# An expert stage whose residual, scaling and final sum move to other engines

## The reference, cut to what matters

```python
x = _layernorm(x + sa, g1, beta1)
t = x.reshape(-1, D)                                  # 1250 x 512
idx = jnp.argmax(t @ Wg + bg, axis=-1)                # one of 8 experts per token
h = jax.nn.gelu(jnp.einsum('td,edh->teh', t, W1) + b1, approximate=False)   # 512 -> 256
y = jnp.einsum('teh,ehd->ted', h, W2) + b2                                  # 256 -> 512
moe = jnp.einsum('ted,te->td', y, one_hot(idx, E))
return _layernorm(x + moe, g2, beta2)                 # and the caller adds x of the stage before
```

## Time and profile before

| | |
|---|---|
| median of 3 runs | 1898.34 us (1892.71 to 1900.72) |
| the profiled execution's own time | 1899.85 us |
| its span | 1898.2 us |
| PE busy | 1765.4 us (93% of the span) |
| PEld busy | 1537.4 us (81%) |
| DVE busy | 1307.2 us (69%) |
| ACT busy | 913.3 us (48%) |
| POOL busy | 591.2 us (31%) |
| the expert stage, from its first load to the end | about 1785.9 to 1898.2 us |

### The profile page before, as it was taken

The page is one execution under the profiler, slowest core; times in us unless marked ns, Lnnn a source line. Parts: engine busy times, 40 slices in busy tenths (PEclk is TensorE's granted clock), DMA queues, the critical chain, the costliest instruction groups (busy, mean ns, idle before and its releaser), DMA issues. The chain is left out here.

```text
span 1898.2 us, 31991 instructions
## 1 busy us (share of the span) xinstructions
PE 1765.4 (93%) x10970; PEld 1537.4 (81%) x10970; DVE 1307.2 (69%) x2964; ACT 913.3 (48%) x1660; POOL 591.2 (31%) x532
## 2 busy tenths in 40 slices
PE   7998999799999999999689999999899999999596
PEld 5776899688888888788578998988688888888585
DVE  6444466688888888377665565545588787887776
ACT  4332266577777776222331243324465555555421
POOL 0000102555556552011101212222254545444344
PEclk9999999899999999999899999999899999999798
DMA  7652677877777775667222049875020202112632
GB/s 246 213 196 77 203 240 250 221 200 204 201 204 198 203 204 142 156 169 186 86 78 73 1 131 162 203 207 182 11 44 1 66 7 58 32 32 71 217 123 89
DMA packets 183532, 265.14 MB, mean 140 GB/s; under 512 B 55852, under 2 KB 102443, under 8 KB 181109
## 3 DMA queue, kind: packets, MB, share of 16 engines
q1 hardware_dynamic: 117839, 169.58, 30.9%
q0 software_dynamic: 49920, 62.94, 12.4%
q10 hardware_dynamic: 15640, 30.90, 6.6%
HBM read 198.55 MB, written 85.86 MB: 150 GB/s over the span
## 5 line engine op out<-in xcount | busy, mean ns | idle before, releaser
L1103 POOL DMA_INDIRECT edge_rows<-xn_store,edge_index x200 | 242.4, 1212 | 173.5 <-PE psum L138 112.3
L2616 POOL TENSOR_TENSOR mprob<-mprob,mrden 125x1250 f32<-125x1250 f32 x80 | 181.6, 2271 | 222.2 <-DVE mrden L2730 221.7
L2645 ACT ACTIVATE mprob<-psum,mbias 125x1250 f32<-125x1250 f32 x80 | 104.3, 1303 | 154.5 <-DVE mbias L2739 154.5
L1321 DVE TENSOR_TENSOR edge_xt_lo<-psum,edge_xt_hi 128x500 fp32r<-128x500 f32 x200 | 134.8, 675 | 59.3 <-ACT edge_xt_hi L1196 59.3
L1196 ACT ACTIVATE edge_xt_hi<-psum 128x500 fp32r<-128x500 f32 x200 | 117.6, 589 | 94.5 <-PE psum L1497 94.5
L2737 DVE TENSOR_REDUCE mmin<-psum 125x1 f32<-125x512 f32 (+1 forms) x240 | 127.0, 584 | 47.4 <-PE psum L2919 47.2
L2937 PE MATMUL psum<-ident,mprob 125*125 125x125 f32 x800 | 117.2, 291 | 17.5 <-DVE ptm_lo L2744 9.4
L2937 PEld LDWEIGHTS psum<-ident,mprob 125*125 125x125 f32 x800 | 99.7, 190 | 35.1 <-DVE ptm_lo L2744 20.4
L2744 DVE TENSOR_TENSOR ptm_lo<-psum,ptm_hi 125x500 fp32r<-125x500 f32 (+1 forms) x240 | 126.4, 582 | 2.0 <-ACT ptm_hi L2651 2.0
L1497 PE MATMUL psum<-ident,edge_rows 125*128 125x125 f32 x800 | 120.2, 273 | 7.6 <-POOLq L1110 5.1
L1350 DVE TENSOR_TENSOR edge_rows_lo<-edge_rows,edge_rows_hi 125x1024 fp32r<-125x1024 f32 x100 | 121.2, 1212 | 0.0
(11 more groups left out here) (530 smaller groups left out, 5355.3 us busy)
## 6 DMA issues: line engine op xcount, KB each, us to landing
slots_in<-blank_rows ACTq DMA_DIRECT2D x20, 1026.0 KB, 16.5
t_store<-t_part SPq DMA_DIRECT2D x20, 1000.0 KB, 5.3
t_row<-t_store SPq DMA_DIRECT2D x47, 400.0 KB, 6.7
y_store<-y_rows SPq DMA_DIRECT2D x50, 200.0 KB
q_chunk<-q_store SPq DMA_DIRECT2D x40, 250.0 KB, 5.3
y_tile<-y_store SPq DMA_DIRECT2D x10, 896.0 KB
edge_attr<-in_attr SPq DMA_DIRECT2D x50, 112.0 KB
moe_xg<-slots_in SPq DMA_DIRECT2D x17, 256.5 KB, 3.0
```

Source lines behind the costliest of these rows:

```text
L1103: nc.gpsimd.indirect_dma_start(xe[t % RING][:, s, :], None, g.xn_store, bass.IndirectOffsetOnAxis(ap=index[t % RING][:, s, 0:1], axis=0)). ...
L1321: nc.vector.tensor_tensor(xt_lo[:, k, :], x_bank(KT * t + k), f32(xt_hi[:, k, :]), ALU.subtract).then_inc(x_low, 1)
L2616: nc.gpsimd.tensor_tensor(prob[:, n % 4, :], prob[:, n % 4, :], rden[:, n % 4:n % 4 + 1].broadcast_to([P, N]), ALU.mult).then_inc(p_ready, 1)
```

## The change

It makes six edits in `expert_mixture`. TensorE no longer adds the tile's own rows: the unit matrix and its eight matmuls per tile go. VectorE does this addition instead, in place in the gathered rows `xg`, ahead of the bn_stats, which now reads SBUF. The rows are turned, and split into halves, two tiles ahead of their use instead of one. VectorE's second row operation (y) goes: ScalarE multiplies by the scale, in place in `y`, and GpSimd adds x3, in place in `y`, ahead of its output DMA. The ring of gathered rows has eight buffers, and a load now also waits until `z_done`, since the rows are needed until then. The scale gets four columns.

```diff
-    RING, OUT, TURNS, LAG = 6, 4, 3, 3
+    RING, OUT, TURNS, LAG = 8, 4, 3, 3
...
+                sp.wait_ge(z_done, i - RING + 1)
...
         def spread_out(i):
+            pool.wait_ge(y_scaled, i + 1)
+            pool.wait_ge(x3_in[i % OUT], 16 * (i // OUT + 1))
+            nc.gpsimd.tensor_tensor(y[:, i % OUT, :], y[:, i % OUT, :], x3[:, i % OUT, :], ALU.add).then_inc(y_done, 1)
             pool.wait_ge(ids_taken, i + 1)
             pool.wait_ge(y_done, i + 1)
...
-                act.wait_ge(o_done, i - TURNS + 1)
+                act.wait_ge(u_done, i - TURNS + 1)
...
+        def scaled(i):
+            act.wait_ge(z_done, i + 1)
+            act.wait_ge(rr_done, i + 1)
+            nc.scalar.activation(y[:, i % OUT, :], y[:, i % OUT, :], ACT.Copy, scale=rr_of(i)).then_inc(y_scaled, 1)
...
-            if i + 1 < TILES:
-                turned_hi(i + 1)
+            if i + 2 < TILES:
+                turned_hi(i + 2)
...
+            if i >= LAG:
+                scaled(i - LAG)
...
         def moments(i):
+            row = xg[:, i % RING, 0:D]
             dve.wait_ge(o_done, i + 1)
-            link(nc.vector.bn_stats(stats[:, i % 2, :], out_bank(i)))
+            nc.vector.tensor_tensor(row, out_bank(i), row, ALU.add).then_inc(o_free, 1)
+            dve.wait_ge(o_free, i + 1)
+            link(nc.vector.bn_stats(stats[:, i % 2, :], row))
...
+            if i >= 4:
+                dve.wait_ge(y_scaled, i - 3)
+            nc.vector.tensor_scalar(rr[:, i % 4:i % 4 + n.stop], rough[:, n], ROOT_SCALE, None, ALU.mult).then_inc(rr_done, n.stop)
...
-            dve.wait_ge(x3_in[i % OUT], 16 * (i // OUT + 1))
-            nc.vector.scalar_tensor_tensor(y[:, i % OUT, :], z[:, s, :], rr[:, s:s + 1], x3[:, i % OUT, :], ALU.mult,
-                                           ALU.add).then_inc(y_done, 1)
+            nc.vector.scalar_tensor_tensor(y[:, i % OUT, :], xg[:, i % RING, 0:D], mv[:, i % 2, 0:1], g2[:], ALU.subtract,
+                                           ALU.mult).then_inc(z_done, 1)
...
-            for k in range(KT):
-                for half in (xt_hi, xt_lo):
-                    nc.tensor.matmul(out[:, k * 128:(k + 1) * 128], half[:, i % TURNS, k, :], unit[:], start=False, stop=False)
             pe.wait_ge(ht_lo_done, i + 1)
...
-            if i + 1 < TILES:
-                turn_rows(i + 1)
+            if i + 2 < TILES:
+                turn_rows(i + 2)
```

More of the change, by code:

```diff
@@ L3047, in expert_mixture @@
     MT = HID // 128
-    RING, OUT, TURNS, LAG = 6, 4, 3, 3
-    xg, x3 = at("moe_xg", [128, RING, ROW], F32, 164), at("moe_x3", [128, OUT, D], F32, 176.25)
+    RING, OUT, TURNS, LAG = 8, 4, 3, 3
+    xg, x3 = at("moe_xg", [128, RING, ROW], F32, 164), at("moe_x3", [128, OUT, D], F32, 180.25)
     xt_hi, xt_lo = at("moe_gt_hi", [128, TURNS, KT, 128], F32R, 84), at("moe_gt_lo", [128, TURNS, KT, 128], F32R, 90)
@@ L3052, in expert_mixture @@
     ht_hi, ht_lo = at("moe_ht_hi", [128, 2, MT, 128], F32R, 78), at("moe_ht_lo", [128, 2, MT, 128], F32R, 80)
-    unit = at("moe_unit", [128, 128], F32R, 82)
-    z, y = at("moe_z", [128, 2, D], F32, 188.25), at("moe_y", [128, OUT, D], F32, 192.25)
+    y = at("moe_y", [128, OUT, D], F32, 192.25)
     g2 = at("moe_g2", [128, D], F32, 200.25)
@@ L3057, in expert_mixture, with rr_of @@
     stats, mv = at("ln2_stats", [128, 2, 6], F32, S), at("ln2_mean_var", [128, 2, 2], F32, S + .0625)
-    ve, rough, hh, rr = (at(n, [128, 2], F32, S + .125 + i / 32) for i, n in enumerate(("ln2_ve", "ln2_r", "ln2_h", "ln2_scale")))
+    ve, rough, hh = (at(n, [128, 2], F32, S + .125 + i / 32) for i, n in enumerate(("ln2_ve", "ln2_r", "ln2_h")))
+    rr = at("ln2_scale", [128, 4], F32, S + .125 + 3 / 32)
+    def rr_of(i):
+        col = 2 * ((i + 1) // 2 % 2) + i % 2
+        return rr[:, col:col + 1]
     out_row, x3_row = at("moe_out_row", [128, TILES], I32, S + .25), at("moe_x3_row", [128, TILES], I32, S + .34375)
@@ L3063, in expert_mixture @@
     pool_steps = sem("moe_rows_steps")
-    g2_in, unit_ready = sem("moe_g2_in"), sem("moe_unit")
+    g2_in, z_done, rr_done, y_scaled = sem("moe_g2_in"), sem("moe_z_done"), sem("moe_rr_done"), sem("moe_y_scaled")
     xg_in, ids_taken = [sem(f"moe_xg_in{i}") for i in range(RING)], sem("moe_ids_taken")
@@ L3111, in scalar @@
     def scalar(act):
-        nc.scalar.activation(unit[:], g.ident[:], ACT.Copy).then_inc(unit_ready, 1)
         def turned_hi(i):
@@ L3131, in scalar @@
             nc.scalar.activation(ht_hi[:, i % 2, :, :], turn_bank(i), ACT.Copy).then_inc(ht_hi_done, 1)
+            if i >= LAG:
+                scaled(i - LAG)
+        for i in range(TILES - LAG, TILES):
+            scaled(i)
     def vector(dve, late_weights):
@@ L3151, in scales @@
             rough_root(nc, link, rough[:, n], ve[:, n], hh[:, n])
-            link(nc.vector.tensor_scalar(rr[:, n], rough[:, n], ROOT_SCALE, None, ALU.mult))
+            if i >= 4:
+                dve.wait_ge(y_scaled, i - 3)
+            nc.vector.tensor_scalar(rr[:, i % 4:i % 4 + n.stop], rough[:, n], ROOT_SCALE, None, ALU.mult).then_inc(rr_done, n.stop)
         def rows_out(i):
-            s = i % 2
             dve.wait_ge(g2_in, 16)
-            nc.vector.scalar_tensor_tensor(z[:, s, :], out_bank(i), mv[:, s, 0:1], g2[:], ALU.subtract,
-                                           ALU.mult).then_inc(o_free, 1)
-            dve.wait_ge(o_free, i + 1)
             if i >= OUT:
                 dve.wait_ge(y_out[i % OUT], 16 * (i // OUT))
-            dve.wait_ge(x3_in[i % OUT], 16 * (i // OUT + 1))
-            nc.vector.scalar_tensor_tensor(y[:, i % OUT, :], z[:, s, :], rr[:, s:s + 1], x3[:, i % OUT, :], ALU.mult,
-                                           ALU.add).then_inc(y_done, 1)
-        turned_lo(0)
+            nc.vector.scalar_tensor_tensor(y[:, i % OUT, :], xg[:, i % RING, 0:D], mv[:, i % 2, 0:1], g2[:], ALU.subtract,
+                                           ALU.mult).then_inc(z_done, 1)
+        turned_lo(0), turned_lo(1)
         for i in range(TILES):
-            if i + 1 < TILES:
-                turned_lo(i + 1)
+            if i + 2 < TILES:
+                turned_lo(i + 2)
             if i == 0:
@@ L3237, in tensor @@
         pe.wait_ge(g.table_ready, 1)
-        turn_rows(0)
-        pe.wait_ge(unit_ready, 1)
+        turn_rows(0), turn_rows(1)
         e_before = None
```

2 lines of the change are left out of this document (1 added, 1 removed).

## The result

The changed kernel took 1906.39 us (median of 7 runs, 1900.05 to 1909.71), the kernel before 1898.34 (median of 7, 1892.71 to 1900.72). The ratio is 1.0042, with a 95% interval of [1.0025, 1.0058]: slower by some 8 us. That is within the 0.5% the prediction called no change, and inside its range, but 5.7 us above its number. A second set of 12 runs gave 1905.82 and 1.0038 [1.0021, 1.0056]. The profiled execution took 1905.46, with a span of 1903.9.

What follows compares the result with a forecast made beforehand. It took a loop of waits between VectorE and TensorE, 10.38 us per two tiles, as the bound. Head, periods and tail, +0.5 - 1.1 + 6 x 0.03 + 0.2 + 2.6 = +2.4, gave 1900.7 us; range 1892 to 1908.

Steps and rivals of the forecast that it cites:

- The old loop: VectorE's bn_stats to moe_gt_lo, then TensorE's product, unit matmuls and second product; said to set 10.38 us per two tiles.
- the new one: Loop of VectorE's hidden-row low part, TensorE's second product, VectorE's addition and bn_stats; bare wait of 1.81 us.
- the period without GpSimd: Two tiles of the changed stage, before any hold of VectorE by GpSimd: 9.96 us.
- I take 0.4: VectorE held by GpSimd's additions at the Newton squares, 0.4 us a period, giving periods of 10.36 to 10.4.
- a page's stronger case: Skill page: one-input fp32 tensor_scalar may use both ports, so + EPS waits too, 0.4 earlier; period 10.8, not used.
- GpSimd's tile of 4.7 in 5.0: GpSimd's work per tile, with addition and two hand-overs of 0.15 to 0.3, takes 4.7 us and just fits 5.0.
- rival A: GpSimd's addition falls wholly into VectorE's Newton chain, 1.29 us a period; +9.0, 1907.3 us; chance 0.13.
- D: TensorE pauses over 2 us each period, clock falls to 1.2 GHz; +27, 1925 us; chance 0.05 with other stalls.
- The tail, +2.6: After the last period, new stations on ScalarE and GpSimd stand uncovered, last output DMA at 9.8; +2.6 us, 2.0 to 3.5.
- The head, +0.5: Stage start: third tile turned before the first product, which moves from 1791.54 to some 1793; +0.5 us, -0.3 to +3.
- B: VectorE is hardly held by GpSimd, period 9.96; -1.8, 1896.5 us; chance 0.15.
- C: Second product not in VectorE's way, VectorE's own work the bound, period 8.75; -8.0, 1890.3 us; chance 0.05.

Runs made afterwards that it cites:

- both_out: Changed kernel without GpSimd's addition of x3 and with four extra bias matmuls per tile on TensorE; ratio 1.0009 to the kernel before.
- ahead: Kernel before with only the rows turned and split two tiles ahead, with four buffers of halves; ratio 1.0000 to the kernel before.
- vec_order: Changed kernel with z of the even tile moved behind the even turn's low part in VectorE's queue; ratio 1.0031 to the kernel before.
- sum_on_te: Changed kernel with the tile's own rows added by TensorE's unit matmuls again; ratio 1.0020 to the kernel before.
- send_later_order: Changed kernel with output DMAs issued one tile later and the even tile's z behind the even turn's low part on VectorE; ratio 1.0001 to the kernel before.
- send_later: Changed kernel with each output DMA issued one tile later on GpSimd; 1906.43 us, ratio 1.0042 to the kernel before.
- filler: Changed kernel with four extra bias matmuls per tile on TensorE, their result overwritten; ratio 1.0042 to the kernel before.
- y_on_vector: Changed kernel with the last scaling and last sum back on VectorE as one operation; ratio 1.0081 to the kernel before.
- order_only: Kernel before with only z and y of the even tile moved behind the even turn's low part on VectorE; ratio 0.9984 to the kernel before.

## Why the prediction was right and wrong

The direction, the range and the verdict of no change were right; the sum was 5.7 us too small. The verdict held by 1.4 us (1906.4 against the 1907.8 at which a change would have been told), and with one term too small by a third and another at nothing it owes something to luck: the stage is 6% of the time and the range was wide. By its steps:

**The old loop is open, and the new one stands bare.** Right. Wait 1.79 for a forecast of 1.81; first period 9.12 for 9.16; the period without GpSimd confirmed by both_out to 0.06, and the two-tiles-ahead part by ahead.

**"I take 0.4" for GpSimd's hold.** The step that failed first, in size and in place. It was 0.38 to 0.94 above the normal 0.17 in every period but the first, +4.4 in all where the sum has 7 x 0.4 = 2.8. The mechanism of the earlier trace rows was right: the operation ends with GpSimd's. But I let it act on the squares with two SBUF inputs only, and left a page's stronger case out of the sum. In every trace with GpSimd's addition the held one is the + EPS, a tensor_scalar with a single SBUF input. No square is, but none shows whether it would be: the + EPS ahead of them absorbs the addition, and no square starts within one. Two SBUF inputs do get held: the z in vec_order that start within an addition take up to 1.41 for 0.75. A single SBUF input by itself does not: bn_stats on SBUF rows, started within an addition 33 times in these traces, always takes 0.69. The Trainium skill says in "VectorE: DVE Perf Modes" (the part on mode 2x_2P) that a one-input fp32 tensor_scalar from SBUF may use both ports; the traces agree in that this operation is held, at 0.53 to 1.14 here. By that sentence alone the period would have been 10.8; three of the kernel after, those without a long wait, are 10.53 to 10.57.

**GpSimd's tile of 4.7 in 5.0.** Wrong. The earlier trace rows gave the parts, but the hand-over from the addition to the DMA is 0.81 and not 0.15 to 0.3, so a tile is 5.17 back to back (sum_on_te). It doesn't fit into a tile's share of 9.96, which is 4.98; rival A's condition held in part. The hold's place depends on it, and vec_order and send_later_order show both directions: with VectorE earlier it grows to 1.75, with GpSimd earlier it falls to 0.53.

**"D and other stalls 0.05".** The second failed step. The argument against was one stretch, with one pause of 2.38 and a granted clock of 0.98. With a pause in every period the clock was at its lower level in four of eight bare products, wholly or from the third matmul on, which cost 0.8 to 1.3 more each, +4.6. What the price is was readable before: the earlier trace rows have a bias matmul at 0.42 for 0.27. What decides which pause is followed by the lower level is not settled: pauses of 3.08, 2.81 and 4.35 were, and 2.76 was not, but in send_later a product behind a pause of 2.48 ran low and others behind 2.94 and 3.07 did not, in vec_order one behind 3.25 did not either, and in filler two fell within the product behind pauses of 1.51 and 1.76. That the low products come with the pauses is shown by filler and both_out (shorter pauses, clock 1.00 in the middle of the stage), and from the other side by y_on_vector (longer pauses, 0.89, 5.6 of its 15 us).

**The tail, +2.6.** The stations were right and so was ScalarE's 0.73 for one row scaling (0.6 to 0.8). The two hand-overs of GpSimd from an addition to its output DMA were not: 0.78 instead of some 0.3 each, so +3.7.

**The head, +0.5.** It was -1.2 in one profile, outside the bounds of -0.3 to +3, and -0.2 in the other. The third turn did come ahead of the first product, from 1790.03. What the bounds missed is when the clock rises: 6.5 us after the first turned rows in the change, 10.4 in the kernel before. Part of that is chance and not the change's: order_only has the head of the kernel before, its clock is up at 7.7, and its head is 12.43 for 13.33.

**Rivals.** A's time, 1907.3, lies nearest to the result, but only a part of its cause was at work: up to 0.94 of its 1.29 a period. B is out, as no trace with GpSimd's addition was without a hold, and C, as the second product stands bare with its 1.79. D, for some of the periods, cost as much as the hold (+4.6 against +4.4). Two slips in the working change nothing: the sum has 6 x 0.03 where the period of 10.36 gives 6 x -0.02, 0.3 us, and C's last period, at 8.75 - 0.60, would be 1.4 under that of before and not 0.2.

## What to carry to other kernels

When a loop of waits is opened, look for the wait that lies bare under it, and move work that the waiting engine has in its own queue into that wait: with both, the period fell from 10.37 to 9.40, while moving whole operations to idle engines gained nothing. An idle engine is not free: before an elementwise operation goes to GpSimd, ask which small operation of VectorE falls beside it, and whether GpSimd's own tile, with its 0.8 behind each addition, fits the period. A matmul engine that is relieved and then pauses in each period can lose more by its clock than the removed matmuls were worth: here 4.6 us against the 0.4 a period, 2.3 us, by which the change shortened the loop.
